# Adaptive-layernorm attention and quantised feed-forward: five pairs of row scales found together in the last stage

## The reference

```python
def _fake_quant_lastdim(x):
    s = jnp.max(jnp.abs(x), axis=-1, keepdims=True) / QMAX      # QMAX = 127
    s = jnp.maximum(s, 1e-08)
    return jnp.clip(jnp.round(x / s), -QMAX, QMAX) * s

def _dyn_quant_linear(x, w, b):
    return jnp.einsum('bti,oi->bto', _fake_quant_lastdim(x), _fake_quant_lastdim(w)) + b

h = _layernorm(vit_embeds, gamma, beta)
h = _dyn_quant_linear(h, w1, b1)
h = jax.nn.gelu(h, approximate=False)
h = _dyn_quant_linear(h, w3, b3)
...
x = x + _L0_attn_ref(_L0_cond_ref(x, ...), ...)
x = x + _L0_ffn_ref(_L0_cond2_ref(x, ...), ...)
```

## Time and profile before

| | |
|---|---|
| median of 3 runs | 559.31 us (554.47 to 561.33) |
| profiled execution, its own time | 560.78 us |
| span of the profiled execution | 558.7 us, mean TensorE clock 0.991 |
| PE busy | 534.9 us (96%) |
| DVE busy | 477.6 us (85%) |
| ACT busy | 429.0 us (77%) |
| POOL busy | 383.3 us (69%) |

### The profile page before, as it was taken

How to read it: one execution, slowest core, us unless ns; L and a number is a source line. 1 busy time by engine, 2 the same in 40 slices (tenths; PEclk the granted TensorE clock), 3 DMA queues, 4 the chain that set the end, 5 groups by cost and what they waited for, 6 DMA issues and landing times.

```text
span 558.7 us, 10860 instructions
## 1 busy us (share of the span) xinstructions
PE 534.9 (96%) x3190; PEld 332.7 (60%) x3190; DVE 477.6 (85%) x629; ACT 429.0 (77%) x1091; POOL 383.3 (69%) x400
## 2 busy tenths in 40 slices
PE   8999979999999999999999999999999999987985
PEld 6744456666666666666666666666666666653442
DVE  4885957999899899989998999899989998876897
ACT  3574558878888888788878887888788878876795
POOL 3005485799779877987799779867986897741063
PEclk9989999999999999999999999999999999999899
DMA  8931344742673267327733672367336532410003
GB/s 295 271 74 38 82 107 133 170 95 57 170 178 88 57 177 175 79 66 177 176 69 75 176 181 61 82 177 168 70 82 169 131 79 72 96 38 1 1 20 132
DMA packets 41341, 63.47 MB, mean 114 GB/s; under 512 B 12452, under 2 KB 20804, under 8 KB 41316
## 3 DMA queue, kind: packets, MB, share of 16 engines
q1 hardware_dynamic: 35652, 46.94, 32.3%
q0 software_dynamic: 3648, 12.75, 11.3%
q10 hardware_dynamic: 2016, 3.48, 2.0%
HBM read 28.55 MB, written 2.10 MB: 55 GB/s over the span
## 4 chain that ended last, share of the span: by engine, by line
PE 82%; DVE 8%; ACT 4%; issue 2%; DMA 2%; POOL 1%; ACTq 0%; SPq 0%; DVEq 0%; POOLq 0%
PE pair L1578 22%; PE pair L1579 22%; PE flow L1702 11%; PE flow L1567 9%; PE flow L1694 6%; PE pair L1485 3%; PE pair L1507 1%; DVE y_max L1361 1%; DMA swap_q<-raw_q 1%; PE flow L1572 1%; DVE accT L1265 1%; ACT probs L779 1%; PE flow L1485 1%; DVE probs L1373 1%; DVE rope_c L1373 1%
## 5 line engine op out<-in xcount | busy, mean ns | idle before, releaser
L1265 DVE SCALAR_TENSOR_TENSOR accT<-pair,so_now,accT 128x1024 f32<-128x1024 f32 x103 | 130.9, 1277 | 19.8 <-PE pair L1579 16.2
L1249 DVE SCALAR_TENSOR_TENSOR raw_q<-pair,sc_now,raw_q 128x1024 f32<-128x1024 f32 x90 | 115.4, 1282 | 7.0 <-ACT raw_q L835 3.9
L572 POOL TENSOR_TENSOR rope_s<-swap_q,consts 128x512 f32<-128x512 f32 x62 | 85.4, 1378 | 30.6 <-DMA swap_q<-raw_q 30.6
L1578 PE MATMUL pair<-ctx_hi,wo 128*128 128x512 f16 x256 | 97.0, 379 | 4.2 <-issue 2.3
L1579 PE MATMUL pair<-ctx_lo,wo 128*128 128x512 f16 x256 | 97.0, 379 | 0.0
L1578 PE MATMUL pair<-h_hi,wq 128*128 128x512 f16 x240 | 91.0, 379 | 0.2 <-ACT raw_q L835 0.2
L779 ACT ACTIVATE probs<-flow,negmax 128x128 f32<-128x128 f32 x248 | 87.3, 368 | 4.9 <-DVE negmax L1217 4.9
L1579 PE MATMUL pair<-h_lo,wq 128*128 128x512 f16 x240 | 91.0, 379 | 0.0
L584 POOL TENSOR_TENSOR qT<-rope_c,rope_s 128x512 f32<-128x512 f32 x62 | 85.5, 1379 | 4.6
L572 POOL TENSOR_TENSOR rope_c<-raw_q,consts 128x512 f32<-128x512 f32 x62 | 77.6, 1274 | 10.7 <-DVE raw_q L1249 10.3
L1702 PEld LDWEIGHTS flow<-probsT,v_now 128*128 128x128 f32 x512 | 62.9, 193 | 19.2 <-ACT probsT L841 15.3
(11 more groups left out here) (281 smaller groups left out, 1008.5 us busy)
## 6 DMA issues: line engine op xcount, KB each, us to landing
swap_q<-raw_q SPq DMA_DIRECT2D x62, 256.0 KB, 3.7
accT<-part_out POOLq DMA_DIRECT2D x22, 512.0 KB, 4.5
wq_i<-in_L_attn_qw_q SPq DMA_DIRECT2D x8, 1024.0 KB, 5.6
wo_i<-in_L_attn_qw_o SPq DMA_DIRECT2D x32, 256.0 KB, 2.8
swap_k<-raw_k SPq DMA_DIRECT2D x14, 256.0 KB, 3.6
wkv_i<-in_L_attn_qw_k SPq DMA_DIRECT2D x8, 256.0 KB, 3.7
wkv_i<-in_L_attn_qw_v SPq DMA_DIRECT2D x8, 256.0 KB, 4.1
stage<-in_x ACTq DMA_DIRECT2D x4, 256.0 KB, 4.7
```

Of the source, the lines that this page charges most:

```text
L572: pool.tensor_tensor(per_seq(into[:, f, :]), per_seq(source[:, f, :]), on_each_seq(table), ALU.mult).then_inc(done, 1)
L1249: dve.scalar_tensor_tensor(out=into, in0=flat(pair[pair_of(h, (kind, j), last, first)][:, :, :]), scalar=sc_now[:, scale_slot(kind, h), j: ...
L1265: dve.scalar_tensor_tensor(out=a, in0=flat(pair[pair_of(h, (O, c), last, first)][:, :, :]), scalar=so_now[:, (h if c == 0 else h - 1) % 2, ...
L1578: pe.matmul(into[:, f, :], w, upper[:, half[f]], start=True, stop=False)
```

## The change

A new helper find_tops(m, b) takes two neighbouring tiles, b and b + 1. It takes both maxima, one after the other, then makes both scales in one instruction of 128x2 and both inverses in a second, and counts top_found[m] up by two at the end. It takes the place of two calls of find_top at five places: (0, 4) with (0, 5), (0, 6) with (0, 7), (1, 2) with (1, 3), (1, 4) with (1, 5), and (1, 6) with (1, 7). Six calls of find_top stay. Where a scale_product stood between the two calls, it now stands ahead of the pair or behind it.

```diff
+            def find_tops(m, b):
+
+                two = slice(b, b + 2)
+                for k in (b, b + 1):
+                    if m:
+                        dve.wait_ge(gelu_done, k + 1)
+                    else:
+                        dve.wait_ge(ln_done, k + 1)
+                    ins = dve.tensor_reduce(y_max[:, m, k:k + 1], y_g[:, k % 2, :] if m else y_ln[k], AX.X, ALU.max, apply_absolute_value=True)
+                link(ins)
+                link(dve.tensor_scalar(y_scale[:, m, two], y_max[:, m, two], 1.0 / QMAX, TINY, ALU.mult, ALU.max))
+                dve.reciprocal(y_inv[:, m, two], y_scale[:, m, two]).then_inc(top_found[m], 2)
...
-            find_top(0, 4)
+            find_tops(0, 4)
             scale_product(0, 1)
-            find_top(0, 5)
             norm(6)
...
```

More of the change, by code:

```diff
@@ L1400, in _ @@
             find_top(1, 1)
-            find_top(0, 6)
             scale_product(0, 4)
-            find_top(0, 7)
+            find_tops(0, 6)
             scale_product(1, 0)
-            find_top(1, 2)
             scale_product(0, 5)
-            find_top(1, 3)
+            find_tops(1, 2)
             scale_product(1, 1)
             scale_product(0, 6)
-            find_top(1, 4)
-            find_top(1, 5)
+            find_tops(1, 4)
             scale_product(0, 7)
@@ L1414, in _ @@
             scale_product(1, 3)
-            find_top(1, 6)
-            find_top(1, 7)
+            find_tops(1, 6)
             scale_product(1, 4)
```

## The result

The changed kernel takes 561.65 us (median of 16 runs, 557.85 to 564.21) against 557.81 us for the kernel before (16 runs, 554.41 to 561.33). The profiled execution took 564.09 us with a span of 562.0 us.

What follows compares the result with a forecast made beforehand. The prediction took DVE and ACT, both full and waiting on each other in a loop, as the bound. Delays reaching 2.99 us at scale_product(1, 6), less 0.05 at the first place, gave 559.31 + 2.9 = 562.2 us, range 557.5 to 566.0.

Steps and rivals of the forecast that it cites:

- the walk through the places: Delays worked out at the five pairs one after another, from distances between starts in the trace: end 2.9 us later.
- What a pair saves: On DVE, a pair takes 1.59 us in place of 1.94, saving 0.35; five save 1.75 us.
- (0, 4) with (0, 5), free: First of the five places: second maximum fits DVE's 0.99 us wait ahead of scale_product(0, 1); a gain of 0.05, dropped.
- (0, 6) with (0, 7): Second place: ACT stands 1.46 us at round(0, 6); DVE then waits 0.86 us at scale_product(0, 5) for gelu(3).
- (1, 2) with (1, 3), (1, 4) with (1, 5): Third and fourth places: round(1, 2) 2.06 us late, round(1, 4) 2.79; DVE waits 1.32 at scale_product(0, 6).
- (1, 6) with (1, 7): Last place: scale_product(1, 6) starts 2.99 us late, including a DVE wait of 0.5 us behind layer(1, 6).
- Rival (1): DVE is the bound, so all 1.75 us saved show at the end: faster, 557.6 us; chance 0.06.
- Rival (2): TensorE's clock falls again between 541 and 552 us, slowing layers: +3.8 to +4.7 us, 563.1 to 564.0; chance 0.10.
- Rival (3): Stands partly overlap with missed slack, and the pairs' saving pays the rest: -0.5 to +1.5 us, about 559.8; chance 0.12.

Runs made afterwards that it cites:

- e10: The changed kernel profiled once more, unaltered: 26.30 us from scale_product(0, 2) to the last addition, where its first profile had 26.85.
- e6: The kernel before with only (1, 4) with (1, 5) and (1, 6) with (1, 7) joined: ratio 1.0021 to the kernel before.
- e9: The changed kernel with gelu(3) and keep(1, 1) ahead of round(0, 6) in ScalarE's order: ratio 1.0056 to the kernel before.
- e5: The kernel before with only (0, 4) and (0, 5) joined, ahead of scale_product(0, 1): ratio 1.0007 to the kernel before.
- e2: The kernel before with only (0, 6) and (0, 7) joined, behind scale_product(0, 4): ratio 1.0007 to the kernel before.
- e1: The changed kernel's VectorE order, but two single find_top calls in place of each pair: ratio 1.0014 to the kernel before.
- e4: The kernel before with each maximum reading 256 of its 512 columns, so its output differs: ratio 0.9982 to the kernel before.
- e12: Against the kernel before: only (0, 6) with (0, 7) and (1, 2) with (1, 3) joined, VectorE's and ScalarE's orders changed: ratio 0.9997.
- e7: The changed kernel with each pair's inverses as two one-column instructions, each counting up by one: ratio 1.0066 to the kernel before.
- e8: The kernel before with single find_top calls reordered so each inverse stands as early as its input allows: ratio 0.9982 to the kernel before.
- e11: The changed kernel with six extra matmuls ahead of layer(0, 7), profiled a second time: 26.30 us from scale_product(0, 2) to the last addition.
- e3: The changed kernel with six extra 512-column matmuls on TensorE ahead of layer(0, 7): ratio 1.0066 to the kernel before.

## Why the prediction was right, step by step

The sign held, and so did the mechanism in the back: +2.9 us forecast, 3.84 us between the medians, +3.75 in the stage at full clock. It was low by 0.8 to 0.9 us, 0.42 of it in the back, 0.34 at the first place, and the 0.05 that had been taken off there. The predicted time of 562.2 lies closer to the measured 561.65 than that, and this is luck: the kernel before came out at 557.81 in the later runs and not at 559.31, which hides the missing part. The range of 557.5 to 566.0 had room for every rival, so it is the walk through the places that bears the prediction out. By its own steps:

- **What a pair saves.** Two maxima 0.60 apart: right (two of them take 1.27 together, so they start 0.60 apart). The inverse was put 0.20 behind the joint scale and comes 0.27 behind it. That is the mis-sized term. A row of the trace before would have given it: the weights' joint scales of 128x2 have their inverses 0.27 behind them too (17.99 to 18.26 us), and I had taken from them only the busy time. A pair takes 1.66 us (in e10 from 535.18 to 536.84) and not 1.59; it saves 0.28 us, not 0.35, and each of the four later places cost some 0.08 more. That a joint scale can take 0.40 us and more, as e6 and e9 show, wasn't foreseen at all.
- **(0, 4) with (0, 5), free.** This step was wrong, by 0.34 us and in its way, shown by e5. The wait of 0.99 us ahead of scale_product(0, 1), into which the second maximum was to fall, came from an execution in which the granted clock had fallen to 0.53 just ahead and layer(0, 0) took 1.91 us. At full clock there is no such wait, and VectorE's own work is the path. The pair makes scale_product(0, 1) 0.68 us late, layer(0, 2) has to wait for it because it writes the same PSUM bank, and of the 0.68 us 0.34 reach scale_product(0, 2). The list of steps ahead of the prediction names keep_yT alone as what a layer waits for; a layer of m = 0 waits for the scale_product of the tile before it as well. The profile's second line of windows told me of the clock; I used it for a rival and not for this step.
- **(0, 6) with (0, 7).** ACT was to stand 1.46 us at round(0, 6): 1.43. DVE was to wait 0.86 at scale_product(0, 5): 0.82. e2 shows the same alone, and e9 takes the wait away.
- **(1, 2) with (1, 3), (1, 4) with (1, 5).** ACT 0.9 at round(1, 2): 0.88. DVE 1.32 at scale_product(0, 6): 1.30. DVE 0.43 at the maximum of (1, 5): 0.29.
- **(1, 6) with (1, 7).** DVE 0.5 at scale_product(1, 6): 0.36. The end of the back 2.99 later: 3.41 (e10). Of the 0.42 between them four times 0.08 is the distance above. The rest is likely the hop to DVE where the gelu is one of two waits: gelu(3) ends at 540.69, and scale_product(0, 5) starts at 540.80, 0.11 later and not 0.04; the chain of waits after has an instruction of DVE's queue in between (L1384, the wait for gelu_done).
- **Rival (1), VectorE's work is the bound,** fell by e1 and e4 for the back; in the front, up to scale_product(0, 1), it is true, as e5 shows. The Trainium skill, Perfetto Trace Analysis, section Optimizing Scalar/DVE Operations, says that grouping into larger operations can improve throughput if the engine is saturated. VectorE, at 4.86 of 5 us, was, and the change lost 3.75 us, the joining alone 2.38. The section also says that breaking up instructions may let work finish sooner where Scalar or Vector aren't saturated but cause bubbles on other engines. Here taking the pairs apart gave those 2.38 us back (e1), in a kernel whose VectorE had been saturated before the change.
- **Rival (2), the clock.** Its sign, a granted clock under 1.00 behind 541 us, did show. The clock fell in the profiled execution at 546 us, and layer(0, 7) took 1.68 us for its usual 1.03 (PE's timeline after):

```profile
546.06 1.68 PE L1849 MATMUL pair<-ffT,y_qT 128*128 128x512 bf16 x4 [1.54 <-DVE rope_c L1386]
```

  It cost little: 26.85 against 26.30 in e10, of which 0.23 is the slow joint scale at 552.84. By e10 and e11 it comes and goes with the execution; nothing ties it to the change.
- **Rival (3), the stands overlap with slack,** is true in part of each place (1.44 us of stand became 1.05 at the end in e2), as the walk had it, but not of the sum.

## What to carry over

Before two small steps are joined to save an engine's time, read how long the consumer of the first result had been waiting for it: here 0.28 us saved delayed a result by 0.6 us and more, on a consumer with 0.16 us of slack, and one pair with its order cost 1.05 us. Joining is safe where the first result isn't wanted yet (e12). Read a second way by which the delay can go: what stands behind the joined steps on their own engine, and who waits for that (e5). A waiting instruction should have nothing behind it in its engine's order that the other engine needs. Check also that the rows for a slack come from a stretch at the clock that the executions usually have.

## What the runs showed of the hardware

- An inverse that counts its semaphore up by two had a semaphore instruction of its own ahead of it and started 0.27 us behind the joint scale; as two inverses that count by one each it was 0.20, and 0.19 in find_top.
- A joint scale of 128x2 took 0.17 us as a rule, but 0.40 (552.84, changed kernel), 0.59 (545.64, e6) and 0.74 us (538.74, e9) once each. Each time a POOL instruction was running when it started, and the scale ended 0.02 to 0.04 us behind that one. In e9 it was add_bias, which ended at 539.45, and the scale at 539.48:

```profile
538.18 1.27 POOL L663 TENSOR_TENSOR rope_c<-rope_c,rows 128x512 f32<-128x512 f32 x1
```

  None of the 36 joint scales in the ten profiles with pairs ended ahead of a POOL instruction that was running when it started, while 71 scales of 128x1 lay wholly inside one and all took 0.15 us. So by the times the joint scale waits for POOL and the single one doesn't. No run moves POOL's instruction alone, and POOL's spans are rough, so the cause isn't shown. The output's transfers don't fit: in e9 the scale had run for 0.26 us before any moved (DMA share 0.00 from 538.74 to 539.00), and in e10 the one at 550.10 took 0.17 under a share of 1.02.
- The granted clock fell to its lower level, 1.2 GHz, for some 3 us at 525 us (before), 546 (changed), 516 and 543 (e7), 517 (e8), 517 and 541 (e11) and 524 (e12), and not at all inside the stage in the other eight profiles. The same kernel is on both sides twice: the changed one fell in its first profile and not in e10, the filler fell in e11 and not in e3.
- The start of norm(0) lay between 516.45 us (e5) and 521.33 us (e6) in executions whose instructions up to there are the same. These 4.9 us are most of the 5.8 between the two executions' own times (556.02 and 561.83). What moves the start wasn't looked into.
